# Attention with routed experts on one core: values matmuls in aligned runs of two key tiles, row sums behind them, and two heads' narrow diagonal score tiles in one step

## The reference

```python
def _L0_attn_ref(x, Wq, bq, Wk, bk, Wv, bv, Wo, bo):
    ...
    logits = jnp.einsum('bqhgd,bkhd->bhgqk', qg, k) * scale
    causal = jnp.tril(jnp.ones((s, s), bool))
    logits = jnp.where(causal, logits, jnp.float32(-1e+30))
    w = jax.nn.softmax(logits, axis=-1)
    out = jnp.einsum('bhgqk,bkhd->bqhgd', w, v).reshape(b, s, NQ * D)
    return out @ Wo + bo
...
h = _layernorm(x, axis=-1) * (1 + ca) + sa
x = x + ga * _L0_attn_ref(h, ...)
h = _layernorm(x, axis=-1) * (1 + cb) + sb
x = x + gb * _L0_ffn_ref(h, ...)
```

## Time and profile before

| | |
|---|---|
| median of 3 runs | 1151.8 us (1147.91 to 1152.04) |
| the profiled execution | 1151.97 us, of which the span is 1150.4 us |
| TensorE (PE) busy | 1070.4 us, 93% |
| VectorE (DVE) busy | 831.7 us, 72% |
| ScalarE (ACT) busy | 553.3 us, 48% |
| GpSimd (POOL) busy | 588.4 us, 51% |

### The profile page before, as it was taken

One profiled execution on the slowest core, in us unless ns is written; L12 is line 12 of the kernel. 1 busy time (PEld: TensorE's weight loads), 2 busy tenths in 40 slices (PEclk: granted clock), 3 DMA queues, 4 the chain that ended last, 5 costly groups with the idle time before them and its releaser, 6 DMA issues.

```text
span 1150.4 us, 16377 instructions
## 1 busy us (share of the span) xinstructions
PE 1070.4 (93%) x5471; PEld 652.4 (57%) x5471; DVE 831.7 (72%) x1948; ACT 553.3 (48%) x1155; POOL 588.4 (51%) x632
## 2 busy tenths in 40 slices
PE   4799999999899999998999999989999989897993
PEld 2456565554565555545555655455556454476992
DVE  5677878776778787767787877687877779763333
ACT  2444544545455455454545454545454345553551
POOL 5554655646356457473365673643544535435441
PEclk9789999999999999999999999999999989988997
DMA  8000000000000000000000000000020002502104
GB/s 235 18 1 1 1 1 1 2 1 1 1 1 1 1 1 1 1 1 1 1 1 1 1 1 1 1 1 1 1 74 1 1 1 91 141 26 81 31 25 123
DMA packets 30019, 25.07 MB, mean 22 GB/s; under 512 B 4481, under 2 KB 25345, under 8 KB 29937
## 3 DMA queue, kind: packets, MB, share of 16 engines
q1 hardware_dynamic: 26224, 18.45, 5.7%
q0 software_dynamic: 2272, 4.72, 1.2%
q10 hardware_dynamic: 1440, 0.85, 0.3%
HBM read 15.62 MB, written 8.40 MB: 21 GB/s over the span
## 4 chain that ended last, share of the span: by engine, by line
PE 73%; DVE 13%; issue 4%; POOL 3%; ACT 3%; DMA 2%; SPq 0%; ACTq 0%; DVEq 0%; POOLq 0%
PE PS L1539 19%; PE PS L1490 12%; PE PS L1521 11%; PE PS L1523 9%; PE PS L1623 3%; PE PS L1465 3%; PE PS L1500 2%; PE PS L1589 2%; PE PS L1472 2%; PE PS L1647 2%; PE PS L1563 2%; DVE full L1134 2%; DVE part_max L1109 2%; DVE PS L1112 1%; DVE full L1161 1%
## 5 line engine op out<-in xcount | busy, mean ns | idle before, releaser
L1109 DVE TENSOR_REDUCE part_max<-PS 128x1 f32<-128x512 f32 x384 | 258.8, 686 | 105.3 <-PE PS L1490 99.5
L879 ACT ACTIVATE full<-PS 128x512 f32<-128x512 f32 x384 | 222.7, 600 | 188.2 <-PE PS L1523 176.3
L1521 PE MATMUL PS<-store 128*128 128x512 f32 (+3 forms) x640 | 264.3, 413 | 3.1 <-ACT full L879 1.2
L1490 PE MATMUL PS<-store 128*128 128x512 f32 (+3 forms) x640 | 249.2, 417 | 8.4 <-ACT store L859 2.8
L1523 PE MATMUL PS<-store 128*128 128x512 f32 (+3 forms) x640 | 235.1, 367 | 0.0
L717 POOL TENSOR_TENSOR full<-full 128x512 f32<-128x512 f32 x120 | 156.0, 1330 | 130.2 <-PE PS L1539 129.2
L888 ACT ACTIVATE diag<-PS 128x512 f32<-128x512 f32 (+3 forms) x256 | 111.6, 442 | 196.2 <-PE PS L1526 158.8
L1490 PEld LDWEIGHTS PS<-store 128*128 128x128 f32 x640 | 118.3, 192 | 141.7 <-issue 49.7
L1539 PE MATMUL PS<-full,V 128*64 128x512 f32 x768 | 191.1, 608 | 0.0
L747 POOL TENSOR_TENSOR lower<-lower 128x320 f32<-128x320 f32 x64 | 60.7, 948 | 244.0 <-DVE lower L1093 241.7
L1521 PEld LDWEIGHTS PS<-store 128*128 128x128 f32 x640 | 122.4, 191 | 85.5 <-ACT full L879 24.6
(11 more groups left out here) (227 smaller groups left out, 1455.2 us busy)
## 6 DMA issues: line engine op xcount, KB each, us to landing
lower<-in_L_ffn_experts_w_dram SPq DMA_DIRECT2D x16, 256.0 KB, 3.9
sent<-full SPq DMA_DIRECT2D x1, 2574.0 KB, 12.2
full<-sent SPq DMA_DIRECT2D x9, 264.0 KB, 4.7
lower<-made SPq DMA_DIRECT2D x8, 256.0 KB, 5.0
full<-in_L_attn_x_dram SPq DMA_DIRECT2D x2, 512.0 KB, 7.1
out_dram<-XA SPq DMA_DIRECT2D x4, 256.0 KB, 2.8
made<-lower,back_to POOLq DMA_INDIRECT x39, 2.2
wo_sb<-in_L_attn_Wo_dram SPq DMA_DIRECT2D x1, 512.0 KB, 10.6
```

The costliest lines, as they stand in the source:

```text
L879: nc.scalar.activation(full[:, k % QUADS, r, :], PS[:, bank, :], ACT.Exp).then_inc(probs_ready, 1)
L1109: nc.vector.reduce_max(part_max[:, t, b:b + 1], PS[:, bank, 0:width], AX.X).then_inc(ring_dve, 1)
L1490: last = nc.tensor.matmul(PS[:, bank, 0:w], QT(ch % 2, h, t * P, (t + 1) * P), keys[:, 0], start=True, stop=True)
L1521: nc.tensor.matmul(o, keys[:, 0], QT(ch % 2, h, q0, BANK), start=True, stop=False)
```

## The change

Three things, all in the planner and in the code of the steps:

1. In `main`, kept values steps go out at even `r`, on the diagonal too, and a gap of 2.1 stands at odd `r`. So tiles 0 and 1 go out together (at `r` = 2), and tiles 2 and 3 at `r` = 0 of the next chunk or pair.
2. `sums_behind_values` moves a `rowsum` to directly behind the next values step that ends at or after its place, with its `norm` and the `out` that follows, unless that would come behind the score step that needs the buffer.
3. `together`: on the diagonal with `r` = 2 or 3 one score step serves both heads. Their 256 or 128 columns each stand side by side in one bank, with two matmuls and one mask matmul for both, and one exponential (L929) writes both.

```diff
--- before.py
+++ after.py
@@ -96,11 +96,21 @@
     N_J = CHUNKS * PAIRS
     LAST = GROUPS * N_J - 1
 
+    def together(J, q, r):
+
+        return q == J % N_J // PAIRS and 2 * (TB - r) <= TB
+
+    def score_step(J, q, r, m):
+
+        return "s", J, q, r, 0 if together(J, q, r) else m
+
     def weight(x):
 
         if x[0] in ("s", "max"):
             _, J, m, t, b = x if x[0] == "max" else (x[0], x[1], x[4], x[3], x[2])
             part = 1.0 if b < J % N_J // PAIRS else ((t + 1) if x[0] == "max" else (TB - t)) / TB
+            if x[0] == "s" and together(J, b, t):
+                part *= 2
             return part * (3.78 if x[0] == "max" else 2.0)
         if x[0] == "gap":
             return x[1]
@@ -144,9 +154,9 @@
         starts.append(len(main))
         for q in range(J // PAIRS + 1):
             for r in range(TB):
-                main += [("s", J, q, r, 0), ("s", J, q, r, 1)]
-                if q < J // PAIRS and r % 2 == 0:
-                    main.append(("gap", 2.1 * len(pending)))
+                main += [("s", J, q, r, 0)] + [("s", J, q, r, 1)] * (not together(J, q, r))
+                if r % 2:
+                    main.append(("gap", 2.1))
                 else:
                     main += pending
                     pending = []
@@ -257,7 +267,45 @@
         order = group_order(*begun, *next_group) if g < GROUPS - 1 else sums_of_last(group_order(*begun, *last_pair))
         at = [(p + g * begin[end], x) for (p, _), x in zip(order, of_group([x for _, x in order], g))]
         placed.append(at)
-    steps += merge(*placed)
+    def local(J):
+
+        return J % N_J // PAIRS
+
+    QUADS = 7
+
+    def quads_in(order):
+
+        owners = []
+        for x in order:
+            if x[0] == "s" and x[3] == 0:
+                _, J, q, _, m = x
+                if q < local(J) or q == 0:
+                    owners += [(J, k, q) for k in range(2)] if together(J, q, 0) else [(J, m, q)]
+        return owners
+
+    def sums_behind_values(placed):
+
+        at = {x: p for items in placed for p, x in items}
+        ends = sorted({p for x, p in at.items() if x[0] == "pv"})
+        owners = quads_in([x for x in merge(*placed)])
+        wanted = {}
+        for old, (J, m, q) in zip(owners, owners[QUADS:]):
+            if old[2] >= local(old[0]) - 1 and q < local(J):
+                p = at["s", J, q, 0, m]
+                wanted[old[0]] = min(p, wanted.get(old[0], p))
+        shift = {}
+        for x, p in at.items():
+            if x[0] == "rowsum" and x[1] not in (LAST - PAIRS, LAST):
+                behind = min(e for e in ends if e >= p)
+                if behind < wanted.get(x[1], behind + 1):
+                    shift[x[1]] = behind + 1e-6 - p
+        return [[(p + shift.get(x[1], 0.0) if x[0] in ("rowsum", "norm") else
+                  p + shift.get(x[1] * PAIRS + PAIRS - 1, 0.0) if x[0] == "out" else p, x) for p, x in items]
+                for items in placed]
+
+    steps += merge(*sums_behind_values(placed))
+    quad_owner = quads_in(steps)
+    quad_of = {key: k for k, key in enumerate(quad_owner)}
 
     SCORES, RING, AV = 0, 2, 6
 
@@ -313,19 +361,6 @@
 
 
 
-    def local(J):
-
-        return J % N_J // PAIRS
-
-    QUADS = 7
-    quad_of, quad_owner = {}, []
-    for x in steps:
-        if x[0] == "s" and x[3] == 0:
-            _, J, q, _, m = x
-            if q < local(J) or q == 0:
-                quad_of[J, m, q] = len(quad_owner)
-                quad_owner.append((J, m, q))
-
     def acc_quad(J, m):
 
         return quad_of[J, m, max(local(J) - 1, 0)] % QUADS
@@ -396,6 +431,10 @@
         def QMT(h):
 
             return area[("QMT", "QMT_last")[h // 2]][:, h % 2 * BANK:(h % 2 + 1) * BANK]
+
+        def QMT_rows(j):
+
+            return area[("QMT", "QMT_last")[j]].rearrange("p (m n) -> p m n", m=2)
 
         FREE_SLOT = GROUPS * CHUNKS % KEY_SLOTS
 
@@ -718,7 +757,7 @@
                             last.then_inc(pool_added, 1)
                             continue
 
-                        pool.wait_ge(probs_ready, n.at["s", J, ch, TB - 1, m] + 1)
+                        pool.wait_ge(probs_ready, n.at[score_step(J, ch, TB - 1, m)] + 1)
                         acc = full[:, acc_quad(J, m)]
                         if ch:
                             pool.wait_ge(pv_done, n.at["pv", J, ch - 1, TB - 1] + 1)
@@ -885,8 +924,14 @@
                         else:
                             act.wait_ge(diag_added, n.at["diagsum", J - 1, m, 1] // 2 + 1)
                     act.wait_ge(scores_ready, n.at[x] + 1)
-                    nc.scalar.activation(diag[:, m, r, r * P:BANK], PS[:, bank, r * P:BANK], ACT.Exp)\
-                      .then_inc(probs_ready, 1)
+                    if together(J, q, r):
+                        w = BANK - r * P
+                        nc.scalar.activation(diag[:, :, r, r * P:BANK],
+                                             PS[:, bank, 0:2 * w].rearrange("p (a n) -> p a n", a=2), ACT.Exp)\
+                          .then_inc(probs_ready, 1)
+                    else:
+                        nc.scalar.activation(diag[:, m, r, r * P:BANK], PS[:, bank, r * P:BANK], ACT.Exp)\
+                          .then_inc(probs_ready, 1)
 
             def round_parts(x):
                 b, ch = x[1] % TB, x[1] // TB
@@ -1137,7 +1182,7 @@
                     ch = local(J)
                     acc = full[:, acc_quad(J, m)]
                     if part == 0:
-                        dve.wait_ge(probs_ready, n.at["s", J, ch, TB - 1, m] + 1)
+                        dve.wait_ge(probs_ready, n.at[score_step(J, ch, TB - 1, m)] + 1)
                         dve.wait_ge(quad_added, n.at["quadsum", J, m, ch - 1, TB - 1] + 1)
                     for r in ((0, 3), (1, 2))[part]:
                         last = nc.vector.tensor_tensor(acc[:, r, r * P:BANK], acc[:, r, r * P:BANK],
@@ -1507,6 +1552,8 @@
                     need(hT_ready, LEAD // TB)
                     taken(("k", J // PAIRS * TB + TB - 1))
                     taken(("qmax", J, m))
+                    if together(J, q, r):
+                        taken(("qmax", J, 1))
                     before = n.scores_before(x)
                     if before is None:
                         slot = n.lent[k % SCORE_BANKS]
@@ -1517,19 +1564,24 @@
                     keys = KT(J // N_J * TILES + q * TB + r)
                     q0 = r * P if q == ch else 0
                     bank = n.score_bank(x)
-                    o = PS[:, bank, q0:BANK]
-                    nc.tensor.matmul(o, keys[:, 0], QT(ch % 2, h, q0, BANK),
-                                     start=True, stop=False)
-                    last = nc.tensor.matmul(o, keys[:, 1], QMT(h)[:, q0:BANK],
-                                            start=False, stop=q < ch)
+                    if together(J, q, r):
+                        w = BANK - q0
+                        o = PS[:, bank, 0:2 * w].rearrange("p (a n) -> p a n", a=2)
+                        corner = o[:, :, 0:P]
+                        high, with_max = QT_rows(ch % 2)[:, J % PAIRS, :, q0:BANK], QMT_rows(J % PAIRS)[:, :, q0:BANK]
+                        mask = causal16[:, 1:2, :].broadcast_to([P, 2, P])
+                    else:
+                        o, corner, mask = PS[:, bank, q0:BANK], PS[:, bank, q0:q0 + P], causal16[:, 1, :]
+                        high, with_max = QT(ch % 2, h, q0, BANK), QMT(h)[:, q0:BANK]
+                    nc.tensor.matmul(o, keys[:, 0], high, start=True, stop=False)
+                    last = nc.tensor.matmul(o, keys[:, 1], with_max, start=False, stop=q < ch)
                     if q == ch:
-                        last = nc.tensor.matmul(PS[:, bank, q0:q0 + P], ident16[:], causal16[:, 1, :],
-                                                start=False, stop=True)
+                        last = nc.tensor.matmul(corner, ident16[:], mask, start=False, stop=True)
                     last.then_inc(scores_ready, 1)
                 elif kind == "pv":
                     _, J, q, r = x
                     ch = local(J)
-                    need(probs_ready, n.at["s", J, q, r, 1] + 1)
+                    need(probs_ready, n.at[score_step(J, q, r, 1)] + 1)
                     if q == 0 and r == 0 and J >= 2:
                         need(attn_ready, n.at["norm", J - 2] + 1)
                     kt = q * TB + r
```

## The result

The changed kernel is slower. Its median is 1165.13 us (1164.20 to 1168.08, 4 runs) against 1151.86 us for the kernel before; the ratio is 1.0127, with a 95% interval of 1.0103 to 1.0151. The forecast was 1121 us. The experiments were timed in several sessions, in which the kernel before had medians of 1149.1 to 1151.9 us; each ratio is to the kernel before of the same session, so kernels of different sessions are compared by their ratios. The profiled execution has a span of 1162.7 us, 12.3 us longer than before's.

The account below looks back on a forecast made before the run. The prediction took PE's own sequence to bound the kernel. Savings of 29.8 (fewer runs) and 8.3 us (joint steps), less 3.2 (added wait) and 4.2 (not realised), gave 30.7 off 1151.97: 1121 us, range 1107 to 1140.

Parts of the forecast that it names:

- I cost this at nothing: Moving a row sum back with its DVE steps, norm and out was claimed to cost nothing, ACT's buffers being guarded.
- The bound of 56 us: Cost if ACT, then PE, waited up to 1.87 us at each of 30 row sums; thought excluded by the guard.
- What bounds the kernel: PE's own sequence, busy 49.61 of 50 us mid-group; time taken from it comes off the whole, except near groups' ends.
- The price of a run: Each run of half-array matmuls costs PE 0.35 us whatever its length; 85 fewer runs save 29.8 us.
- The bound downward: Only a run's ending, 0.15 us, is saved if entering and leaving were hidden by other waits: 12.8 us.
- Joint steps: Two heads in one narrow score step save PE 0.26 us in each of 32 pairs, 8.3 us; bounds 0 and 21.
- The added wait: The joint step with r = 2 waits for head 0's exponential: 3.2 us back, bounds 0 and 11 us.
- What is not realised: Some tenth of the runs lies where PE isn't full: 4.2 us back, bounds 0 and half of 38.1.
- DVE taking over: DVE runs late, the ring's banks fill and PE waits, losing half the saving: 1133 to 1146 us, chance 0.13.
- Joining giving nothing: Each key tile in a run still pays its own entry and end, leaving 1144 us; chance 0.04.
- Exponentials on the path: Each of 64 joint steps waits 0.85 us for an exponential, two score banks being too few: 1168 us, chance 0.04.
- Doesn't do what it says: Fewer, longer runs just wait longer, or later row sums hold the buffers: 1146 to 1157 us, chance 0.05.

Follow-up runs that it names:

- no_row_sums: The changed kernel with row sums left at their own places, aligned runs and joint steps kept: 1149.86 us, 1.0008 of the kernel before.
- joint_only: The kernel before with joint score steps alone, values steps and row sums as they were: 1145.75 us, ratio 0.9971.
- pool_after_norm: The changed kernel without moved row sums, with POOL's additions of the 31st pair waiting until DVE's normalising is done: 1139.96 us, ratio 0.9912.
- aligned_only: The kernel before with aligned runs of values steps alone, row sums and score steps as they were: 1155.19 us, ratio 1.0059.
- light_after: The changed kernel with off-diagonal maxima taken over 128 keys instead of 512, leaving out part of DVE's work: 1141.28 us, ratio 0.9903.
- early maxima: The changed kernel with the `max` steps of each group's second to fifth pairs planned 0.07 to 0.1 pair earlier: 1149.83 us, ratio 0.9994.
- no_joint_steps: The changed kernel without joint score steps, aligned runs and moved row sums kept: 1168.35 us, 1.0166 of the kernel before.

## Why the prediction was wrong

**The failed step** is one line of the second part: moving a row sum also moves its DVE steps and `out`, "I cost this at nothing". The cover named for it was on ACT's side (the buffers), and that one held but for little: ACT waits for row sums in 3 places as before, 9.0 us in place of 3.2. The one that mattered is on DVE's queue: the maxima stand behind the row sum's steps, and `qmax` on PE stands behind the maxima. PE's waits there went from 7.4 to 28.5 us, the clock was lower behind four of them, and in place of the 9.5 us (27 runs) that moved row sums were to gain they cost 13.7. The bound of 56 us was priced for ACT and thought excluded.

**What bounds the kernel** was right in the middle of a group and too coarse for the whole. Every engine of this kernel walks its list in order, and in the first pairs of a group PE waits at `qmax` for DVE, which waits for PE's row sum; there an average of 72% for DVE says nothing.

**The price of a run** was right where PE hardly waits, and too high over the whole. In the changed kernel a run of two still takes 1.87 us from start to start:

```profile
588.67 1.94 PE L1591 MATMUL PS<-full,V 128*64 128x512 f32 x8
590.54 0.50 PE L1535 MATMUL PS<-store 128*128 128x512 f32 x1
```

In the fifth to seventh pairs of the third group PE's busy time is 113.7 us before and 110.3 in `no_row_sums`, 3.4 less; 7 runs fewer and the joint steps give 7 x 0.35 + 3 x 0.26 = 3.2. Over the eight pairs of the group, all at the full clock, it is 229.5 and 224.2 us, 5.3 less, where 15 runs fewer and the joint steps give 15 x 0.35 + 8 x 0.26 = 7.3; the joint steps alone brought 2.2 (227.4 in `joint_only`). So a run saved brought 0.35 us where PE is full, but some 0.2 over the group. The bound downward had named a reason, entering and leaving hidden by other waits; no run shows that it is this one.

The page's totals can't settle it. In `pool_after_norm` PE's busy time is 1042.6 us, 27.8 below the kernel before and close to the sum's 58 x 0.35 + 8.3 = 28.6; in `no_row_sums`, with the same runs and joint steps, it is 1048.4, 22.0 below. The mean granted clocks are 0.979, 0.971 and, before, 0.973, so the closeness of the first is luck.

A row sum behind two values steps costs what was said: from 573.39 to 575.90 is 2.51 us, and 0.86 + 0.86 x 0.75 (384 columns) + 0.86 + 0.15 gives 2.52. Even so the other 27 runs, those of the row sums, brought 1.4 us of busy time in the page (1047.0 against 1048.4) where 9.5 were counted. The lower clock hides part of it: at 0.50, 1.7 us in each of three groups, against 1.7 less of it elsewhere. In the third group, with the clock's 1.7 us taken off, 7 runs fewer brought 0.9 us where 2.5 were counted; the rest stays open.

**Joint steps** were right in kind: 3.3 us gained against 8.3 less 3.2 and about 1.0 for three runs, so 6.1. PE's busy time fell by 10.4 us, as forecast (9.3). The added wait was smaller than priced, 1.8 us at L933 in the changed kernel; `joint_only` lost the rest as waits at other places, of which `qmax` shows 1.8 us (9.2 against 7.4).

**"What is not realised"**, 4.2 us, was the second step that failed, by as much as the first. It took the places where PE waits as a share of the runs that bring nothing. In fact taking work from PE moved steps of the engines against each other: PE's time without work in the third group rose from 4.6 to 7.6 us without moved row sums and to 10.5 with them. And in the last group it moved DVE's normalising beside POOL's additions (nine take 8.33 us in `no_row_sums` and 8.32 in `aligned_only`, 2.39 before and 2.40 in `joint_only`), which cost 10 us as `pool_after_norm` shows. No row of the kernel before was read for POOL, although the 1.27 and 1.17 us shown above stood in its trace.

**The rivals.** DVE taking over was judged by load, and its sign was the weights' wait over 42 us; that wait fell to 26.7, so it isn't DVE's share of the time. It was latency in DVE's order, ahead of one kind of step, for which there was no rival; DVE's work is part of that latency, as `light_after` shows. Joining giving nothing is refuted by the 1.87 us, which is less than 2 x 1.01, and by the busy time of `aligned_only`, 15.6 us less at nearly the same mean clock (0.974 against 0.973) with aligned runs alone. With it goes the rule on weight loads by which it would have held (the Trainium skill, page "TensorE: Matmul & The Clock Gate", section "Part 3: Packing small matmuls — row/col tiling"), which the earlier trace rows already spoke against. Exponentials on the path didn't happen. "Doesn't do what it says" had row sums hold the buffers, which cost ACT the 9.0 us above and not more, and ended at 1157 us. A time above 1157 us had 0.04 by another mechanism, waits for exponentials, whose 1168 us lies near the measured time by luck; the range failed by 25 us.

**The account of 1165 us**, by differences of the ratios times 1152: joint steps -3.3, aligned runs on top of them +4.3, moved row sums +13.7; together 14.7 us, where the forecast had -30.7. Of these 45 us the moved row sums make 23 (13.7 in place of -9.5) and the aligned runs 24 (4.3 in place of 55 x 0.35 = -19.3); the joint steps make 3, and the 4.2 set aside goes the other way. POOL's wait takes 11.1 us off, so that aligned runs without the overlap give 4.3 - 11.1 = -6.8. The 12.5 us that are still missing are found in part in the third group: from `joint_only` to `no_row_sums` PE's work there falls by 3.1 us, where 14 runs were to give 4.9, and its time without work grows by 1.9. What lies behind either was not isolated.

**Not tried:** moved row sums with early maxima and POOL's wait together, which by these numbers might lie near `pool_after_norm`; early maxima without moved row sums; and POOL's wait in `joint_only`.

## What to carry to other kernels

When a step is moved on one engine, write down what stands behind its companion steps in every other engine's queue, and who waits for that; a step costed "at nothing" needs the row of the cover on each of them. Judge in-order engines by the last wait at a place, not by load over a stretch, and read the granted clock behind a long wait of PE: here 2.48 us without work cost another 1.7 in some places and nothing in others. After a change that shifts engines against each other, look for instructions whose duration, not whose wait, changed: the 8.33 us appear in the list of waits as PE waiting for `part_max`, not under their own cause.

## What the hardware showed that was not expected

Some of DVE's SBUF instructions are held to POOL's pace when both engines run: nine TENSOR_SCALAR of 128x128 took 8.33 us beside POOL's additions and 2.39 us alone. POOL lost nothing: six additions took 7.41 us beside them and eight took 9.89 us alone, 1.24 us each. Others kept their time: twelve BATCH_NORM_AGGREGATE took 0.91 us beside POOL in `no_row_sums` (918.72) and 0.91 alone in `pool_after_norm`. DVE's maxima from PSUM go on beside POOL's additions at 0.69 us each, as elsewhere. The Trainium skill, page "SBUF — State Buffer", section "SBUF: two separate sides", says that DVE, in a 2-port mode or with two inputs in SBUF, and GpSimd need one pair of ports, held as an exclusive lock, and that the loser "fully blocks". The trace agrees for the instructions that were slowed, with 1299 ns in place of 335 as the number; in which mode they ran no row here shows.

PE's granted clock was at 0.50 from 544.0 to 547.5 us, from 1 us after PE took up work again behind the wait of 2.48 us; around the wait of 1.33 us at the end of the third pair, 577 to 585 us, it stayed at 1.00. The same wait of 2.48 us was followed by the lower clock in all three groups shown of the changed kernel, and in one of three in `no_joint_steps`.
